# A second expert layer's tiles: row tiles stream over copied weights instead of weights streaming over row tiles

## The reference

```
logits = x @ gate_w.T ; scores = softmax(logits)
topk_w, topk_i = top_k(scores, 2)            # 8 experts
topk_w = topk_w / (sum + 1e-20) * 2.5
g = silu(x @ w_gate[e]) * (x @ w_up[e])      # 128 -> 176
expert_out = g @ w_down[e]                   # 176 -> 128
y = sum over picks of topk_w * expert_out
x = x + y + shared_swiglu(x)                 # 128 -> 352 -> 128
```

## Time and profile before

| | |
|---|---|
| median of three executions | 452.03 us (449.4 to 454.14) |
| span of the profiled execution, first to last instruction | 429.2 us |
| median less that span | 22.8 us |
| mean granted TensorE clock | 0.942 of full |
| busy in the span: PE, PEld, DVE, ACT, POOL | 87%, 63%, 65%, 58%, 46% |
| first load of a tile's rows issued | 343.19 us |
| first and last scatter of a tile's results start | 353.32 and 418.60 us |

### The profile page before, as it was taken

How to read it: one execution, slowest core, us unless ns; L and a number is a source line. 1 busy time by engine, 2 the same in 40 slices (tenths; PEclk the granted TensorE clock), 3 DMA queues, 4 the chain that set the end, 5 groups by cost and what they waited for, 6 DMA issues and landing times.

```text
span 429.2 us, 10202 instructions
## 1 busy us (share of the span) xinstructions
PE 375.2 (87%) x2637; PEld 270.4 (63%) x2637; DVE 278.9 (65%) x1132; ACT 247.4 (58%) x743; POOL 197.5 (46%) x273
## 2 busy tenths in 40 slices
PE   4999999899999995799998998479988779899960
PEld 4456556556666652689998997145565457677650
DVE  4566888888878888376555666369566536365562
ACT  2688788788887891546555564328874124344420
POOL 5421254444334434544554555223737506466561
PEclk9999999999999996599999999569999999899995
DMA  7603999678888404467767675320101122232354
GB/s 150 95 15 97 391 279 251 165 166 199 195 204 182 89 20 136 113 160 180 215 165 199 173 175 155 106 94 21 57 26 52 48 52 72 69 79 76 81 172 147
DMA packets 61072, 57.14 MB, mean 133 GB/s; under 512 B 6042, under 2 KB 49703, under 8 KB 60768
## 3 DMA queue, kind: packets, MB, share of 16 engines
q1 hardware_dynamic: 56288, 48.10, 45.1%
q0 software_dynamic: 4736, 8.47, 5.8%
HBM read 36.12 MB, written 21.73 MB: 135 GB/s over the span
## 4 chain that ended last, share of the span: by engine, by line
PE 58%; issue 12%; DMA 9%; DVE 8%; POOL 6%; ACT 4%; SPq 1%; POOLq 1%; DVEq 0%; ACTq 0%
PE bank L764 13%; PE bank L773 6%; PE bank L896 5%; PE bank L787 5%; PE bank L901 5%; DMA layer_outputs<-w_all 3%; POOL layer_outputs L744 3%; PE bank L1023 3%; DMA w_all<-layer_rows 2%; POOL layer_outputs L702 2%; PE bank L1103 2%; DMA qexp<-layer_outputs 2%; PE bank L804 2%; PE bank L818 2%; PE bank L871 2%
## 5 line engine op out<-in xcount | busy, mean ns | idle before, releaser
L1151 ACT ACTIVATE ps<-bank,ntop 128x128 f32<-128x128 f32 x256 | 73.4, 378 | 11.8 <-DVE ntop L1414 10.1
L1218 ACT ACTIVATE hT<-bank,w 128x128 f32<-128x128 f32 x176 | 50.8, 368 | 40.4 <-PE bank L896 40.1
L764 PE MATMUL bank<-qexp 128*128 128x512 f32 x128 | 67.8, 612 | 0.5 <-ACT ps L1151 0.5
L744 POOL DMA_INDIRECT layer_outputs<-w_all x40 | 39.9, 997 | 39.1 <-DVE w_all L1917 21.7
L773 PEld LDWEIGHTS bank<-ident,ps 128*128 128x128 f32 x256 | 31.9, 141 | 33.3 <-issue 29.8
L896 PE MATMUL bank<-xT,w 128*128 128x128 f32 x352 | 49.1, 284 | 2.8 <-DMA w<-in_L_ffn_w_dram 1.2
L1160 ACT ACTIVATE pT<-bank 128x512 f32<-128x512 f32 x64 | 38.6, 603 | 19.1 <-PE bank L773 18.1
L1413 DVE TENSOR_REDUCE mx<-bank 128x4 f32<-128x512 f32 x64 | 43.7, 683 | 8.5 <-PE bank L764 7.0
L668 POOL TENSOR_TENSOR qexp<-kA,rowmask 128x512 f32<-128x512 f32 x15 | 15.6, 1037 | 69.1 <-DVE kA L1498 69.1
L896 PEld LDWEIGHTS bank<-xT,w 128*128 128x128 f32 x352 | 44.6, 199 | 4.0 <-issue 2.6
L732 POOL DMA_INDIRECT layer_rows<-rows_all,places x32 | 30.8, 961 | 24.7 <-DVE rows_all L1791 10.3
(11 more groups left out here) (328 smaller groups left out, 814.6 us busy)
## 6 DMA issues: line engine op xcount, KB each, us to landing
w<-in_L_ffn_w_dram SPq DMA_DIRECT2D x44, 258.0 KB, 3.4
layer_rows<-fill SPq DMA_DIRECT2D x10, 910.0 KB, 9.1
w_all<-in_L_ffn_w_dram SPq DMA_DIRECT2D x24, 256.0 KB, 4.7
qexp<-layer_outputs SPq DMA_DIRECT2D x8, 512.0 KB, 4.0
xt<-layer_rows SPq DMA_DIRECT2D x45, 65.0 KB
w_all<-layer_rows SPq DMA_DIRECT2D x40, 65.0 KB, 1.9
xfT<-in_xfT_dram SPq DMA_DIRECT2D x16, 128.0 KB, 2.4
layer_rows<-fill SPq DMA_DIRECT2D x1, 1560.0 KB, 12.3
```

Source lines behind the costliest of these rows:

```text
L744: g.indirect_dma_start(ys1_dram, bass.IndirectOffsetOnAxis(ap=xt1[r][:, P:P + 1].bitcast(U32), axis=0), yb1[r][:, :], None, bounds_check=Y ...
L764: pe.matmul(psA[g % 2][:, :], qexp[b % 2][:, g, :], kexp[b % 2].rearrange("p g k -> p (g k)"), start=True, stop=True).then_inc(a_in_ps, 1)
L1151: m = s.activation(ps[g % 2][:, t, :], psA[g % 2][:, t * P:(t + 1) * P], ACT.Exp, bias=ntop[:, h:h + 1])
L1218: s.activation(hT[r % 2][:, c, :], banks[c][:, 0:P], ACT.Gelu, bias=w1[r][:, F0 + c:F0 + c + 1]).then_inc(gelu_done, 1)
```

## The change

Only the second layer's expert tiles and what prepares them are changed.

- The up multiplication is the other way round: the weights are held in the array and the turned rows move through. Three multiplications of 128 columns take the place of one of 352: gate columns 0 to 127, up columns 0 to 127, and the remaining 48 of each together, with gaps of zeros. The hidden tile comes out with features along the partitions, so it need not be turned again, and `turn_hidden1` and ScalarE's copy are gone.
- VectorE copies each tile's up weights (128 x 384) and down weights (128 x 256) from the expert's place to one of two fixed buffers each, `wgu1_r` and `wd1_r`. TensorE's addresses are constants.
- The expert words are read into VectorE's registers, the five of them at three places inside the shared network's last block. SyncE reads all 14 place words before its first tile load.
- ScalarE takes over the copy of the turned rows, makes two silus a tile, and scales the results of even tiles; VectorE multiplies in two pieces and scales those of odd tiles.
- There are 16 row slots instead of 8; the result slots stay 8. The wait for scatters reaches back 16 tiles, and a wait for the load eight tiles back is added.
- TensorE's order is `up1(j)`, `turn_tile1(j+2)`, `down1(j-2)`. There are 39 tiles instead of 40.

```diff
-TILES1 = B * P * 2 // P + E1
+TILES1 = B * P * 2 // P + E1 - 1
+TABLE1 = TILES1 + 1
+ROWS1 = 16
...
             sp.wait_ge(plan1_ready, 1)
+            places = [sp.value_load(place1[0:1, n:n + 1], min_val=0, max_val=256 ** 3 - 1) for n in range(WORDS1)]
             sp.wait_ge(filled, 16 * FILLS)
             sp.wait_ge(rows_sent, 16 * 2 * B)
...
-                if j % 3 == 0:
-                    word = sp.value_load(place1[0:1, j // 3:j // 3 + 1], min_val=0, max_val=256 ** 3 - 1)
                 if n > 0:
-                    sp.wait_ge(y1_sent[r], 16 * n)
-                m = clamped((word // 256 ** (j % 3)) % 256, XS_TILES - 1)
-                sp.dma_start(xt1[r][:, :], xs1_j[bass.ds(m, 1)].rearrange("o p d -> (o p) d")).then_inc(xt1_in[r], 16)
+                    sp.wait_ge(xt1_in[r], 16 * n)
+                if n > 1:
+                    sp.wait_ge(y1_sent[r], 16 * (n - 1))
+                m = clamped((places[j // 3] // 256 ** (j % 3)) % 256, XS_TILES - 1)
+                sp.dma_start(xt1[j % ROWS1][:, :], xs1_j[bass.ds(m, 1)].rearrange("o p d -> (o p) d")).then_inc(xt1_in[r], 16)
...
-                pool.wait_ge(yb1_ready, j + 1)
+                pool.wait_ge(yb1_ready[j % 2], j // 2 + 1)
...
             def up1(j):
-                e = expert(j)
+                w = wgu1_r[j % 2]
+                pe.wait_ge(w1_kept, j + 1)
                 pe.wait_ge(xT1_ready, j + 1)
                 if j >= 2:
-                    pe.wait_ge(ht1_ready, j - 1)
-                pe.matmul(banks[2 + j % 2][:, 0:2 * F1], xT1[j % 2][:, :], wgu1[:, bass.ds(e, 1), :].rearrange("p o f -> p (o f)"),
-                          start=True, stop=True).then_inc(gu1_in_ps, 1)
-
-            def turn_hidden1(j):
...
+                    pe.wait_ge(hT1_ready, j - 1)
+                pe.matmul(banks[4 + j % 2][:, 0:P], w[:, 2 * P:3 * P], xT1[j % 2][:, :], start=True, stop=True).then_inc(rest1_in_ps, 1)
+                pe.matmul(banks[2 + j % 2][:, 0:P], w[:, 0:P], xT1[j % 2][:, :], start=True, stop=True)
+                pe.matmul(banks[2 + j % 2][:, P:2 * P], w[:, P:2 * P], xT1[j % 2][:, :], start=True, stop=True).then_inc(gu1_in_ps, 1)
...
             turn_tile1(0)
+            turn_tile1(1)
             for j in range(TILES1 + 2):
                 if j < TILES1:
                     up1(j)
-                if j + 1 < TILES1:
-                    turn_tile1(j + 1)
-                if 0 <= j - 1 < TILES1:
-                    turn_hidden1(j - 1)
+                if j + 2 < TILES1:
+                    turn_tile1(j + 2)
                 if j >= 2:
                     down1(j - 2)
...
+            for j in range(TILES1):
+                silus1(j)
+                if j + 2 < TILES1:
+                    keep_xT1(j + 2)
+                if j >= 2 and j % 2 == 0:
+                    result1(j - 2)
...
+            def keep_weights1(j):
+                if j >= 2:
+                    dve.wait_ge(gu1_in_ps, j - 1)
+                v.tensor_copy(wgu1_r[j % 2], wgu1[:, bass.ds(expert(j), 1), :].rearrange("p o f -> p (o f)")).then_inc(w1_kept, 1)
+
+            def keep_down1(j):
+                if j >= 2:
+                    dve.wait_ge(y1_in_ps, j - 1)
+                v.tensor_copy(wd1_r[j % 2], wd1[:, bass.ds(expert(j), 1), :].rearrange("p o d -> p (o d)")).then_inc(wd1_kept, 1)
...
             shared_sum(2)
+            read_words(0, 1)
             shared(3, 1)
+            keep_weights1(0)
+            keep_weights1(1)
+            read_words(2)
             shared(3, 2)
+            read_words(3, 4)
             shared_sum(3)
...
+            def hidden1(j):
+                dve.wait_ge(silu1_done, 2 * j + 1)
                 if j >= 2:
-                    dve.wait_ge(hT1_in_ps, j - 1)
...
+                    dve.wait_ge(y1_in_ps, j - 1)
+                v.tensor_tensor(hT1[j % 2][0:FR, P:2 * P], sg1[j % 2][0:FR, P:2 * P], banks[4 + j % 2][0:FR, 0:P], ALU.mult)
+                dve.wait_ge(silu1_done, 2 * j + 2)
+                v.tensor_tensor(hT1[j % 2][:, 0:P], sg1[j % 2][:, 0:P], banks[2 + j % 2][:, P:2 * P], ALU.mult).then_inc(hT1_ready, 1)
...
             for j in range(TILES1 + 2):
-                if j + 1 < TILES1:
-                    turned1(j + 1)
                 if j < TILES1:
                     hidden1(j)
-                if j >= 2:
+                    keep_down1(j)
+                if j + 2 < TILES1:
+                    keep_weights1(j + 2)
+                if j >= 2 and j % 2 == 1:
                     result1(j - 2)
```

More of the change, by code:

```diff
@@ L39 @@
 FR = F1 - P
+UP1 = 3 * P
+GAP1 = 64
 NSH = [(0, 128), (128, 128), (256, 96)]
@@ L120, in attention_moe_kernel @@
         vB = second_w[0:A1, A1 + E1 + 2 * FS:]
-        wgu1 = sb("wgu1", [P, E1, 2 * F1])
-        wda1 = sb("wda1", [P, E1, P])
-        wdb1 = sb("wdb1", [P, E1, P])
+        wgu1 = sb("wgu1", [P, E1, UP1])
+        wd1 = sb("wd1", [P, E1, 2 * P])
         wsd = sb("wsd", [P, len(NSH), P])
@@ L262, in attention_moe_kernel @@
         wordp1 = sb("wordp1", [1, WORDS1])
-        wordf1 = sb("wordf1", [1, TILES1 // 8])
+        wordf1 = sb("wordf1", [1, TABLE1 // 8])
         sg = [part(9 + i) for i in range(2)]
         hsh = [part(11 + c) for c in range(NS1)]
-        xt1 = [late[:, 16 * W + RW * r:16 * W + RW * (r + 1)] for r in range(RING1)]
-        yb1 = [late[:, 16 * W + RW * RING1 + P * r:16 * W + RW * RING1 + P * (r + 1)] for r in range(RING1)]
-        xT1 = [part(22)[:, P * i:P * (i + 1)] for i in range(2)]
-        ht1 = [spare[:, 1024 + 256 * i:1280 + 256 * i] for i in range(2)]
+        xt1 = [late[:, 16 * W + RW * r:16 * W + RW * (r + 1)] for r in range(ROWS1)]
+        yb1 = [late[:, 16 * W + RW * ROWS1 + P * r:16 * W + RW * ROWS1 + P * (r + 1)] for r in range(RING1)]
+        xT1 = [late[:, 16 * W + RW * ROWS1 + P * (RING1 + i):16 * W + RW * ROWS1 + P * (RING1 + i + 1)] for i in range(2)]
+        assert 16 * W + RW * ROWS1 + P * (RING1 + 2) <= 23 * W
+        wd1_r = [spare[:, 2 * UP1 + 2 * P * i:2 * UP1 + 2 * P * (i + 1)] for i in range(2)]
+        wgu1_r = [spare[:, UP1 * i:UP1 * (i + 1)] for i in range(2)]
         hT1 = [spare[:, 1536 + 256 * i:1792 + 256 * i] for i in range(2)]
-        sg1 = [spare[:, 2048 + 256 * i:2048 + 256 * i + F1] for i in range(2)]
+        assert 2 * UP1 + 4 * P <= 1536
+        sg1 = [spare[:, 2048 + 256 * i:2304 + 256 * i] for i in range(2)]
         w_att = sem("w_att")
@@ L383, in attention_moe_kernel @@
         xt1_in = [sem(f"xt1_in{r}") for r in range(RING1)]
+        wd1_kept = sem("wd1_kept")
         xT1_in_ps = sem("xT1_in_ps")
         xT1_ready = sem("xT1_ready")
+        rest1_in_ps = sem("rest1_in_ps")
         gu1_in_ps = sem("gu1_in_ps")
         silu1_done = sem("silu1_done")
-        ht1_ready = sem("ht1_ready")
-        hT1_in_ps = sem("hT1_in_ps")
         hT1_ready = sem("hT1_ready")
         y1_in_ps = sem("y1_in_ps")
-        yb1_ready = sem("yb1_ready")
+        yb1_ready = [sem(f"yb1_ready{i}") for i in range(2)]
+        w1_kept = sem("w1_kept")
         y1_sent = [sem(f"y1_sent{r}") for r in range(RING1)]
@@ L1082, in _ @@
             shared_down(3)
-            words = [None] * (TILES1 // 8)
-            def expert(j):
-                if words[j // 8] is None:
-                    words[j // 8] = pe.value_load(words1[0:1, j // 8:j // 8 + 1], min_val=0, max_val=8 ** 8 - 1)
-                return (words[j // 8] // 8 ** (j % 8)) % 8
             def turn_tile1(j):
@@ L1853, in _ @@
             bend(0)
-            for t in ht1:
-                v.memset(t[:, F1:2 * P], 0.0).then_inc(ht1_zero, 1)
-            dve.wait_ge(ht1_zero, 2)
+            for t in hT1:
+                v.memset(t[:, P:2 * P], 0.0).then_inc(hT1_zero, 1)
+            dve.wait_ge(hT1_zero, 2)
             mixing(1)
@@ L1891, in _, with read_words, expert @@
             order_tiles(1)
+            words = []
+            def read_words(*which):
+                for n in which:
+                    words.append(dve.value_load(words1[0:1, n:n + 1], min_val=0, max_val=8 ** 8 - 1))
+            def expert(j):
+                return (words[j // 8] // 8 ** (j % 8)) % 8
+            def keep_weights1(j):
+                if j >= 2:
+                    dve.wait_ge(gu1_in_ps, j - 1)
+                v.tensor_copy(wgu1_r[j % 2], wgu1[:, bass.ds(expert(j), 1), :].rearrange("p o f -> p (o f)")).then_inc(w1_kept, 1)
+            def keep_down1(j):
+                if j >= 2:
+                    dve.wait_ge(y1_in_ps, j - 1)
+                v.tensor_copy(wd1_r[j % 2], wd1[:, bass.ds(expert(j), 1), :].rearrange("p o d -> p (o d)")).then_inc(wd1_kept, 1)
             shared(3, 0)
```

86 lines of the change are left out of this document (43 added, 43 removed).

## The result

The changed kernel takes 457.1 us (median of 20 runs, 451.67 to 461.23), the kernel before 453.73 (20 runs, 448.97 to 456.17). The ratio is 1.0054, with an interval from 1.0029 to 1.0079. Executions more than 1.5% above the fastest of their kernel are left out of every ratio, which is why it is smaller than 457.1 / 453.73. By the 1% that the prediction set, that is no change. 443.5 us and "faster" were wrong.

A forecast was written before the change was run, and what follows sets the result against it. It took TensorE's 1.51 us a tile and the ring of eight row slots as bounds. A loop gain of 14.4 us, less 0.6 + 0.5 and 4.8 at the start, made 452.03 - 8.5 = 443.5 us, range 437 to 452.5.

The forecast's parts named there:

- First scatter: POOL's first scatter of results in the second layer: at 358.15 instead of 353.32 us, 4.8 us given back.
- word reads: SyncE's 14 place words before its first tile load: 0.58 us each, 8.1 us, rows 3.5 us late.
- the 2 us for the clock: TensorE's longer idle stretch before its first turn halves the clock for a while: 2.0 us, ends 0 and 4.
- 38 steps: The tile loop from first to last scatter of results: 38 steps of 1.34 us, 50.9 us.
- Tail: After the last scatter starts: its landing, the last block's load, two sums and the output, unchanged at 10.6 us.
- POOL's part: POOL's scatters in the tile loop: 1.28 us a tile when nothing keeps POOL waiting, the slowest step.
- Copies beside scatters: VectorE's weight copies slow POOL's scatters in the tiles: 0.06 us added, 1.34 us a tile, ends 1.28 and 1.52.
- about 0.1 for three hand-overs: Hand-overs between engines in VectorE's two-tile loop: about 0.1 us of 2.5 us, 1.25 us a tile.
- the ring: Eight row slots made tile loads wait behind scatters, 34.8 us, 0.16 us a tile; sixteen remove the stalls.
- rival 3: Both copies hold up each scatter in the tiles: 1.76 us a tile, 459.5 us; chance 0.09 with the skill's case.
- rival 2: Every scatter starts inside a copy: 1.52 us a tile, 450.5 us; chance 0.22 together with Rival 4.
- Rival 4: Eight result slots close the same ring, so row slots don't matter; ends near rival 2, chance almost nothing.

The follow-up runs named there:

- before_again: The kernel before, unchanged, run once more for a second profile: one execution, 447.08 us.
- fixed_weights: The changed kernel without copies of weights, TensorE reading a fixed expert's weights in turn where they lie: 453.65 us, ratio to before 1.004.
- slots_only: The kernel before with sixteen row slots instead of eight and nothing else of the change: 449.12 us, ratio to before 0.997.
- no_scatters2: The changed kernel without its 39 scatters of results, POOL only marking each as sent: 436.59 us, ratio to before 0.966.
- both_gaps_384: The changed kernel with POOL fills of 384 columns, not waited for, after each row scatter and each scatter of results: 435.98 us, ratio to before 0.974.
- after_both_gaps: The changed kernel with 128-column POOL fills, not waited for, after each row scatter and each scatter of results: 450.20 us, ratio to before 1.009.
- tiles_spaced: The changed kernel with a 128-column POOL fill, waited for, after each scatter of results: 464.61 us, ratio to before 1.043.
- rows_gap: The kernel before with a 128-column POOL fill, not waited for, after each of the 32 row scatters: 447.91 us, ratio to before 1.002.

## Why the prediction was wrong

Against before_again, whose time lies among those of the timed runs, the profiled span grew by 7.2 us (452.5 less 445.3; by the ratio of the runs it is some 2.4, so the sizes below are those of two single executions). The terms, forecast and measured:

- **First scatter:** forecast 4.8 us later, measured 0.1 (369.72 against 369.61). The word reads were right: 7.8 us for 8.1, and the first load 5.2 us later for 5.1. But the first turn came 1.9 us later (363.37 against 361.52) instead of 3.5, since in before_again it stood behind the shared network's last sum (360.73) long after its rows had landed. From the turn to the first scatter 6.35 us went by, 1.7 less than in before_again, whose clock fell there too (0.52 of full from 366 to 368 us), so that the 2 us for the clock were no difference.
- **38 steps:** forecast 13.3 us less (with block bounds and last scatters), measured 6.8 more (72.2 against 65.4). This is the term that failed.
- **Tail:** 10.6 us, as forecast (452.5 less 441.92).

The step that failed is the pace, 1.34 us a tile from "POOL's part" and "Copies beside scatters", and under it the "about 0.1 for three hand-overs" of VectorE's loop. The pace holds only "when nothing keeps POOL waiting", and the hand-overs were put at 0.1 us whatever POOL does. Measured, a single hand-over from TensorE to VectorE took 2.46 us in the rows shown, and POOL's wait of 2.64 us at 403.26 follows it. The other parts were right in themselves. The compute loop alone takes 1.30 us (forecast 1.25). The copies take 0.35 and 0.28 us (0.36 and 0.29). The scatter's price beside copies was 0.06 us forecast and 0.07 measured: 1.051 us here, against 0.979 in fixed_weights and 0.985 in slots_only:

```profile
L747 POOL DMA_INDIRECT layer_outputs<-w_all x40 | 39.4, 985 | 46.0 <-DVE w_all L1920 32.7 <-issue 13.4
```

What was missing is that a scatter may delay a third engine. I looked for what copies do to a scatter, and the harm runs from the scatters to TensorE's reports: without scatters none is late (no_scatters2), without copies they stay (fixed_weights), with the same scatters 1.61 us apart they go (both_gaps_384). It is the distance and not the fill: the same fill of 128 columns leaves them where scatters stay 1.35 us apart (after_both_gaps) and takes them away where a wait makes it 2 us (tiles_spaced). That much is shown, for executions like the timed ones; in the first profile of the kernel before the same close scatters did no harm. How it sets the pace is only the reading that fits: a quicker loop feeds POOL faster, POOL's scatters close up into a train, the reports stop until the train runs dry, and then all engines start anew. The kernel before, with 1.51 us a tile on TensorE, feeds POOL more slowly, and its late results are fewer and shorter (four over 1 us, at most 1.5); so the change may gain on TensorE and lose the same again in trains. This was argued, not tried by itself.

A second step was wrong: "the median of the runs stands 22.8 us above the profiled span; with the same distance". The distance is 1.8 us, in both kernels. The rest of it was a warning that the profile shown is not what the runs do. With it went the reading of the ring: its stalls, 34.8 us in that profile, are 10.8 in before_again, and taking them away gains nothing (slots_only, 0.997).

Of the numbered rivals, rival 3 came nearest in pace, 1.76 us a tile, for the wrong reason; rival 2, which ends within the 1%, had 1.52. By the rule of the Trainium skill, page "SBUF — State Buffer", section "Who interferes with whom", a tile would have taken 1.93 us, close to the 1.90 measured. That is a coincidence: fixed_weights has no copies from SBUF to SBUF in its tiles and is no faster, so the port pair of VectorE and GpSimd isn't what cost the time. Rival 4 did not show in the changed kernel: none of its waits for a result slot is put down to a scatter.

Open is what between POOL's scatters and TensorE's reports is shared, whether TensorE's results or only the news of them come late, and why the first profile of the kernel before shows row scatters 1.26 us apart and no late report. Open is too how much of both_gaps_384's gain is the change's: the kernel before with gaps of 384 columns wasn't run. Between its profile and that of before_again only 1.5 us lie in the tiles.

## What to carry to other kernels

Set the profiled time beside the timed runs before working from it; where they differ by more than runs do among themselves, take another profile first. Where a loop of several engines should get faster, ask what the faster loop does to the engine that was not its bound: here, by the reading above, its transfers closed up and held back others' signals. Compare the record of an instruction's end with the start of the one that waits for it, and if a gap opens there, take away one engine's work at a time, as a whole; a pause in the right place can be quicker than none.

## What the hardware showed that was not expected

In every profile without added gaps but the first, while indirect scatters of 128 rows follow each other on POOL at 1.26 to 1.35 us, engines can start late on TensorE's results: VectorE by 2.5 and 2.6 us in the rows shown, ScalarE by 1.4. At 1.61 us this is gone. The Trainium skill, in the section named above, says among its rules on SBUF's ports that TensorE never waits on anyone. The rows shown don't speak against it: TensorE goes on to the next tile at 399.27 while VectorE still waits for the product that ended at 398.82. A fill of 128 columns costs POOL 0.22 us by itself (mean in rows_gap), and 0.77 us more until the next scatter starts where POOL's queue waits for it.
